# First expert layer in tiles of 128 rows instead of 256, rows standing in the array, second product in F32

## The reference, cut to what matters

```python
H, I, E, TOPK = 256, 688, 8, 2
logits = xf @ router_w.T
top_vals, top_idx = jax.lax.top_k(logits, TOPK)
top_w = jax.nn.softmax(top_vals, axis=-1)
combine = jnp.sum(jax.nn.one_hot(top_idx, E, dtype=xf.dtype) * top_w[..., None], axis=1)
for e in range(E):
    h = jax.nn.silu(xf @ Wg[e].T) * (xf @ Wu[e].T)
    y = h @ Wd[e].T
    out = out + combine[:, e:e + 1] * y
```

## Time and profile before

| | us |
|---|---|
| median of 3 runs | 1885.77 (1878.61 to 1891.75) |
| profiled execution, time | 1884.27 |
| profiled execution, span | 1882.5 |
| mean granted TensorE clock over the span | 0.932 of 2.4 GHz |
| TensorE busy | 1668.8 (89%) |
| VectorE busy | 1283.6 (68%) |
| ScalarE busy | 763.4 (41%) |

### The profile page before, as it was taken

One profiled execution on the slowest core, in us unless ns is written; L12 is line 12 of the kernel. 1 busy time (PEld: TensorE's weight loads), 2 busy tenths in 40 slices (PEclk: granted clock), 3 DMA queues, 4 the chain that ended last, 5 costly groups with the idle time before them and its releaser, 6 DMA issues. The chain is left out here.

```text
span 1882.5 us, 29054 instructions
## 1 busy us (share of the span) xinstructions
PE 1668.8 (89%) x9602; PEld 1163.0 (62%) x9602; DVE 1283.6 (68%) x2381; ACT 763.4 (41%) x1996; POOL 930.2 (49%) x815
## 2 busy tenths in 40 slices
PE   5999978999999999999999968899999289978890
PEld 4677744555555556555555644899999267755780
DVE  5688767777777777877777545687777756665333
ACT  3100103444444444444444423566665156642220
POOL 0477747777777788887775530232331000000536
PEclk9999978999999999999999986899999599988895
DMA  6434352212222222122220002765662420000343
GB/s 192 131 69 97 68 143 79 71 56 66 76 76 76 76 76 63 49 76 76 76 72 10 14 23 93 202 206 191 197 192 95 156 57 0 0 12 28 110 116 105
DMA packets 92020, 168.14 MB, mean 89 GB/s; under 512 B 45729, under 2 KB 70533, under 8 KB 87085
## 3 DMA queue, kind: packets, MB, share of 16 engines
q1 hardware_dynamic: 84077, 147.41, 26.6%
q0 software_dynamic: 7808, 19.02, 3.8%
HBM read 134.91 MB, written 29.53 MB: 87 GB/s over the span
## 5 line engine op out<-in xcount | busy, mean ns | idle before, releaser
L896 ACT ACTIVATE R<-banks 128x400 f32<-128x400 f32 x768 | 326.6, 510 | 318.1 <-PE banks L930 317.3
L712 DVE TENSOR_REDUCE PM<-banks 128x2 f32<-128x964 f32 x320 | 360.9, 1133 | 137.3 <-PE banks L689 137.2
L750 POOL TENSOR_TENSOR EA<-EA,R 128x400 f32<-128x400 f32 x288 | 306.1, 1063 | 118.8 <-ACT R L896 105.4
L930 PE MATMUL banks<-QS,KH 128*128 128x400 f32 x768 | 288.9, 376 | 2.6 <-DMA QB<-ML 2.6
L930 PE MATMUL banks<-QB,KB 128*128 128x400 f32 x768 | 265.6, 346 | 0.0
L730 DVE TENSOR_TENSOR banks<-banks,R 128x400 f32<-128x400 f32 x320 | 183.8, 574 | 27.9 <-ACT R L896 26.7
L539 POOL TENSOR_TENSOR arena<-arena 96x400 f32<-96x400 f32 x128 | 141.4, 1125 | 116.4 <-DVE arena L514 116.1
L182 PE MATMUL banks<-e_xh,e_split 128*116 128x256 f32 x960 | 194.5, 286 | 3.9 <-DVE e_xl L1702 3.9
L940 PE MATMUL banks<-R,KV 128*64 128x400 f32 x960 | 187.5, 512 | 0.0
L930 PEld LDWEIGHTS banks<-QS,KH 128*128 128x128 f32 x768 | 145.2, 189 | 54.7 <-issue 38.4
L689 PE MATMUL banks<-KH,QS 64*128 64x482 f32 x320 | 160.4, 502 | 17.2 <-DVE PM L712 7.7
(11 more groups left out here) (285 smaller groups left out, 3452.2 us busy)
## 6 DMA issues: line engine op xcount, KB each, us to landing
m_stage_u<-in_m_up SPq DMA_DIRECT2D x20, 1392.0 KB
arena<-in_ctx_T SPq DMA_DIRECT2D x16, 1444.0 KB, 6.2
m_stage_d<-in_m_down SPq DMA_DIRECT2D x20, 696.0 KB
QS<-queries SPq DMA_DIRECT2D x16, 800.0 KB, 6.6
queries<-q_out_h SPq DMA_DIRECT2D x64, 100.0 KB, 2.4
queries<-q_out_l SPq DMA_DIRECT2D x64, 100.0 KB, 2.4
QB<-queries SPq DMA_DIRECT2D x16, 400.0 KB, 8.4
arena<-recips SPq DMA_DIRECT2D x32, 200.0 KB
```

The lines of the kernel that those rows point to most:

```text
L712: nc.vector.tensor_reduce(PM[:, 2 * i:2 * i + n], banks[:, k:k + n, 0:KW], AX.X, ALU.max).then_inc(red_done, 1)
L750: nc.gpsimd.tensor_tensor(out, first, tile_of(n, 1), ALU.add).then_inc(odd_sum, 1)
L896: nc.scalar.activation(tile_of(n, o), psum[ring_bank(score_tile(b, n, o))][:, 0:CH], ACT.Exp).then_inc(exp_done, 1)
L930: last = nc.tensor.matmul(out, lhs[r][:, keys], heads[:, o], start=lhs is KH, stop=lhs is KB)
```

## The change

The first expert layer works in tiles of 128 rows (`TOK0`), so `most_tiles(8, 128)` = 32 tiles, each with one gather and one scatter of 128 rows. Each tile still loads its expert's up and down weights whole, in one DMA each, of unchanged shape; there are now three buffers of each. The rows (high and low) stand in the array and the up weights move, 348 of a projection's 696 columns at a time ("halves", index c): per tile 2 halves x 2 projections x 2 x 3 = 24 matmuls of 348 columns. ScalarE and VectorE split the up weights in four pieces per tile. The hidden values, 128 rows x 348, come out in F32 with rows on partitions, are turned by 6 transposes per tile, are moved to SBUF by ScalarE in F32 (`hidden_out`), and stand in the array against the unsplit F32 down weights (6 F32 products of 256 columns per tile). The splits of the down weights and of the hidden values are gone. The diff, cut to its core (`...` marks what is left out):

```diff
+TOK0 = P
...
 class GatedWeights:
-    BUFS, NU, TR, NT = 2, 2, 116, 6
+    BUFS, NU, TR, NT = 3, 2, 116, 6
...
-            d = Dispatch(core, ctx, stage, dram, "m0_", X, ident, E0, TOK, False, normed)
+            d = Dispatch(core, ctx, stage, dram, "m0_", X, ident, E0, TOK0, False, normed)
...
+    tag, U, PARTS = "e0_", 2, 2
+    PT, PC = NT // PARTS, TR * NT // PARTS
+    UB, TB, XB, YB = 0, NU * PARTS, NU * PARTS + PARTS, NU * PARTS + PARTS + 1
...
+        def stage_part(k, i):
+            return stage_u[k % BUFS][:, i % KD, :, part_of(i // KD)]
...
+        UPS = KD * PARTS
...
             def _(sp):
-                def load(k, u):
+                def up_of(k):
                     e = weights.expert_of(sp, d.tile_expert, k)
                     if k >= BUFS:
-                        sp.wait_ge(ul_ready, k + 1)
-                    weights.load_up(sp, e, u)
+                        sp.wait_ge(ul_ready, (k - BUFS + 1) * UPS)
+                    weights.load_up(sp, e, k)
+                    return e
+
+                def down_of(k, e):
                     if k >= BUFS:
-                        sp.wait_ge(dl_ready, k * NT + NT)
-                    weights.load_down(sp, e, u)
-
-                sp.wait_ge(x_in[0], 32)
+                        sp.wait_ge(down_done, (k - BUFS + 1) * PARTS)
+                    weights.load_down(sp, e, k)
+
+                sp.wait_ge(x_in[0], 16)
+                e = up_of(1)
                 for k in range(1, tiles):
-                    load(k, k % BUFS)
+                    following = up_of(k + 1) if k + 1 < tiles else None
+                    down_of(k, e)
+                    e = following
...
             def _(pe):
...
+                def up(k, c):
+                    pe.wait_ge(xl_ready, k + 1)
+                    pe.wait_ge(ul_ready, k * UPS + (c + 1) * KD)
+                    if k >= 1:
+                        pe.wait_ge(h_ready, (k - 1) * PARTS + c + 1)
+                    u = k % U
                     for n in range(NU):
-                        last = split_products(nc, psum[(u * NT + t) % HB][0:TR, n * TOK:(n + 1) * TOK],
-                                              [(UH[u][:, q, n, cols], UL[u][:, q, n, cols], xh[u][:, q, :], xl[u][:, q, :])
+                        last = split_products(nc, psum[UB + c * NU + n][:, 0:PC],
+                                              [(xh[u][:, q, :], xl[u][:, q, :], UH[u][:, q, n, part_of(c)], UL[u][:, q, n, part_of(c)])
                                                for q in range(KD)])
                     last.then_inc(up_ready, 1)
...
+                def turn_hidden(k, c):
+                    pe.wait_ge(h_ready, k * PARTS + c + 1)
+                    if k >= 1:
+                        pe.wait_ge(ht_ready, (k - 1) * PARTS + c + 1)
+                    for t in range(PT):
+                        last = nc.tensor.transpose(psum[TB + c][0:TR, t * TOK0:(t + 1) * TOK0], HF[:, c, t * TR:(t + 1) * TR], ident[:, :])
+                    last.then_inc(hid_turned, 1)
+
+                def down(k, c):
+                    pe.wait_ge(ht_ready, k * PARTS + c + 1)
+                    if c == 0:
+                        pe.wait_ge(down_in[k % BUFS], k // BUFS * 16 + 16)
+                        if k >= 1:
+                            pe.wait_ge(y_done, k)
+                    u = k % U
+                    for t in range(c * PT, (c + 1) * PT):
+                        last = nc.tensor.matmul(psum[YB][:, 0:D], HT[u][:, t, :], stage_d[k % BUFS][:, t, :], start=t == 0, stop=t == NT - 1)
                     last.then_inc(down_done, 1)
...
+                for k in range(tiles):
+                    up(k, 0)
+                    if k >= 1:
+                        turn_hidden(k - 1, 1)
+                        down(k - 1, 0)
+                    up(k, 1)
+                    if k + 1 < tiles:
+                        turn(k + 1)
+                    if k >= 1:
+                        down(k - 1, 1)
+                    turn_hidden(k, 0)
...
             def _(act):
...
+                for k in range(tiles):
+                    following = k + 1 < tiles
+                    if following:
+                        for i in range(KD):
+                            weights_high(k + 1, i)
+                    gate(k, 0)
+                    if k >= 1:
+                        hidden_out(k - 1, 1)
+                    if following:
+                        for i in range(KD, UPS):
+                            weights_high(k + 1, i)
+                    gate(k, 1)
+                    if following:
+                        rows_high(k + 1)
+                    hidden_out(k, 0)
```

More of the change, by code:

```diff
@@ L1532, in gated_experts, with part_of, split_part @@
         added = core.sem(tag + "added")
[L1534 to L1543, removed]
+        def part_of(c):
+            return slice(c * PC, (c + 1) * PC)
+        def stage_part(k, i):
+            return stage_u[k % BUFS][:, i % KD, :, part_of(i // KD)]
+        def split_part(W, k, i):
+            return W[k % U][:, i % KD, :, part_of(i // KD)]
+        UPS = KD * PARTS
         with nc.Block() as block:
@@ L1570, in send @@
                 def send(k):
[L1571 to L1574, removed]
+                    pool.wait_ge(y_done, k + 1)
+                    pool.indirect_dma_start(results[:, :], bass.IndirectOffsetOnAxis(d.target[:, k:k + 1], 0),
+                                            ys[k % U][:], None).then_inc(stored[k % U], 16)
                 for k in range(1, XBUFS):
@@ L1608, in up @@
                     last.then_inc(up_ready, 1)
[L1610 to L1620, removed]
-                    last.then_inc(down_done, 1)
@@ new lines, in _ @@
+                turn(0)
+                for k in range(tiles):
[9 more added lines that the diff above has]
+                    turn_hidden(k, 0)
+                k = tiles - 1
+                turn_hidden(k, 1)
+                down(k, 0)
@@ L1660, in step @@
[L1660 to L1667, removed]
-                        act.wait_ge(h_ready, k * NT + (HB + t + 1))
-                        act.wait_ge(down_done, k * NT + (t + 1))
-                        nc.scalar.activation(HH[u][:, t, :], HF[:, (u * NT + t) % HB, :], ACT.Copy).then_inc(hh_ready, 1)
-                    for t in range(NT + 1):
-                        if t < NT:
-                            gate(t)
-                        if t >= 1:
-                            high(t - 1)
-                        if not is_last(k):
-                            un, mn = next_of(u, m)
-                            for part in range(KD + 1):
-                                if ACT_AT[part] == t:
-                                    weights_high(k + 1, un, mn, part)
-                            if t == 2:
-                                rows_high(k + 1, un)
@@ L1685, in _, with weights_high @@
-                ACT_AT = (0, 1, 3)
-                for part in range(KD):
-                    weights_high(0, 0, 0, part)
-                rows_high(0, 0)
-                weights_high(0, 0, 0, KD)
-                steps(act, step)
+                def weights_high(k, i):
+                    if i == 0:
+                        act.wait_ge(up_in[k % BUFS], k // BUFS * 16 + 16)
+                        if k >= U:
+                            act.wait_ge(up_ready, (k - U + 1) * PARTS)
+                    nc.scalar.activation(split_part(UH, k, i), stage_part(k, i), ACT.Copy).then_inc(w_hi, 1)
@@ new lines, in _ @@
+                for i in range(UPS):
+                    weights_high(0, i)
+                rows_high(0)
+                for k in range(tiles):
[4 more added lines that the diff above has]
+                    gate(k, 0)
+                    if k >= 1:
+                        hidden_out(k - 1, 1)
[6 more added lines that the diff above has]
+                    hidden_out(k, 0)
@@ L1752, in _, with rows_low @@
[L1752 to L1760 removed]
+                def rows_low(k):
+                    v.wait_ge(xh_ready, k + 1)
+                    nc.vector.tensor_tensor(xl[k % U][:], psum[XB][:, 0:KD * TOK0].rearrange("p (k t) -> p k t", k=KD),
+                                            as_f32(xh[k % U][:]), ALU.subtract).then_inc(xl_ready, 1)
@@ new lines, in sums_out @@
+                def sums_out(k):
+                    v.wait_ge(down_done, (k + 1) * PARTS)
+                    if k >= U:
+                        v.wait_ge(stored[k % U], k // U * 16)
+                    nc.vector.tensor_copy(ys[k % U][:], psum[YB][:, 0:D]).then_inc(y_done, 1)
+                for i in range(KD):
+                    weights_low(0, i)
+                rows_low(0)
+                for i in range(KD, UPS):
+                    weights_low(0, i)
+                for k in range(tiles):
+                    following = k + 1 < tiles
+                    if following:
+                        for i in range(KD):
+                            weights_low(k + 1, i)
+                    hidden(k, 0)
```

(9 more changed lines are left out.)

182 lines of the change are left out of this document (52 added, 130 removed).

## The result

The changed kernel takes 2006.05 us (median of 4 runs, 1999.26 to 2008.85) against 1883.48 for the kernel before: 1.0641 times as long, 95% interval 1.0592 to 1.0689. The profiled execution took 1999.26 us with a span of 1997.5, 115 us more than the one of before.

The account below looks back on a forecast made before the run. Four DMA engines carrying the down loads bound it: 6.9 + 4.0 + 0.8 to 0.9, with loss 12.9 us a tile; 1 + 31 x 12.9 + 8 = 409 us, 114 more than before, 1998 us; range 1945 to 2025.

Parts of the forecast that it names:

- The bound of the kernel before: First expert layer: four full DMA engines, with TensorE close behind, set the period of 13.6 to 14.0 us.
- The price of the down load: One tile's 696 KB down load on its four DMA engines: at 103 GB/s, 6.9 us.
- The loss of 1.1 us a tile: Four engines, kernel before: the period's missing 1.1 to 1.4 us, taken as loss where queues alternate; assumed again after.
- TensorE's work: First expert layer after the change: 7.4 us a tile, 32 tiles, 236 us, against 263 us before.
- The chain inside a tile: Gate, `rows_high`, `rows_low` after the second up half: some 1.4 us plus hand-overs, covered by TensorE's other work.
- The cap of 8.1 us for compute: First expert layer after the change: compute alone would go at 7.4 to 8.1 us a tile.
- rival 1: Down loads take four other engines each time; compute decides at 8.1 us a tile: 1861 us, chance 0.06.
- The third buffer: Weight loads: depth adds no capacity, as the four engines already had a queue with two buffers; it keeps them fed.
- Rival 2: Loads slower than compute but cheaper than forecast, 10.5 to 11.8 us a tile: about 1945 us, chance 0.09.
- Rival 3: TensorE's clock falls towards 1.2 GHz when it idles, priced at 14 us a tile: 2032 us, chance 0.08.
- Rival 4: Only splitting and matmuls are halved, not loads; effects cancel at 9.2 us a tile: 1884 us, chance 0.05.
- the signs: Loop after the change: up loads every 12.7 to 13.4 us, DMA share 0.5 to 0.6, TensorE busy under 65%.

Follow-up runs that it names:

- padded kernel before: The kernel before the change, with down weights padded with zero rows from 116 to 128 partitions: 1867.98 us, 0.9942 times the kernel before.
- the run with half the weights: The changed kernel loading only slices 0 to 2 of each tile's down weights, used twice, on 116 partitions: 1886.67 us in one run.
- the padded kernel: The changed kernel with down weights padded with zero rows from 116 to 128 partitions, three buffers: 1836.73 us, 0.9758 times the kernel before.
- the two DMAs of 58 partitions: The changed kernel with each down load issued from SP as two DMAs, partitions 0 to 57 and 58 to 115: 2178.85 us in one run.

## Why the prediction was right

The forecast was 1998 us, from 12.9 us a tile on four full DMA engines. Measured: 2006.05, and 1999.26 in the profiled execution, with 12.76 us a tile.

- The bound of the kernel before. That four engines, and not TensorE alone, set its pace was argued from stretches at 0.31 and 0.26 with loads outstanding. The padded kernel before shows it: 13.25 us a tile instead of 13.6 to 14.0, and 12 us less; and the four are never without a packet in the 230 us. TensorE stood closer than was said: 108 x 0.12 + 0.44 is 13.4 us, not the 13.1 written, and 13.25 is measured.
- The price of the down load, 6.9 us on its four engines: half of it measured 3.6 for 3.45 in the run with half the weights. On two engines 118 partitions would by this price take 14.0 us, 7.1 more; measured from first queued load to read back they cost 200.7 us for 31 tiles, 6.5. What shrinks there is the loss: (607.0 - 9)/31 = 19.3 us a tile, against 14.0 + 4.0 + 0.85 = 18.9.
- The loss of 1.1 us a tile. 11.8 of the 12.76 us are explained by the uncontended prices, 0.96 remain. It is no idle time, since the four always have a packet in flight; it lies in longer packets, on average 0.29 us for one of a down load in the loop against 0.24 in tile 0's, alone. That queues taking turns lengthen them was only argued; two buffers, with less in the queue, lost slightly less (399.7 us from first load to read back against 406.3), which fits but doesn't show it. The term itself was taken over from the kernel before (1.1 to 1.4 us), and that it would be the same after the change had no other ground.
- TensorE's work, 7.4 us a tile: 7.28 measured, in the padded kernel, where nothing hides it. VectorE 5.1 us (139.46 x 7.28 / 200) and ScalarE 4.8 (130.70 x 7.28 / 200) a tile, priced 5.2 and 5.3.
- The chain inside a tile was said to be covered, and the padded kernel, with TensorE busy 200 of 200 us, shows it to be so. The cap of 8.1 us for compute was too careful, which is why rival 1's 1861 us would have been too high by 24.
- The third buffer was said to add nothing to the changed kernel, and adds nothing; that it is worth 20 us once the engines are free was not seen.
- Rival 1 (other engines each time) falls with the two DMAs of 58 partitions and with the packets of the changed kernel. The Trainium skill's rule that the prediction named ("DMA: Bandwidth & Descriptors", section "Why a DMA increments its semaphore by 16 and not by 1"), that a load from SP takes the lowest-numbered engines, agrees in that they are the same ones each time; that they are the lowest no trace shows. Rival 2 (the loss vanishes) had 11.8 us a tile as its upper end; 12.76 is above it. Rival 3's mechanism is there, and costs nothing: in the stretch at clock 0.50 six F32 instructions span 2.93 us instead of 1.46,

```profile
1380.85 2.93 PE L1626 MATMUL banks<-m_stage_d,e_HT 116*128 116x256 f32 x6 [2.52 <-ACT e_HT L1672]
```

but the four engines are never without a packet meanwhile, so nothing is lost by it. Rival 4 is true in its first half: the loads move whole.
- Two of the signs were missed by a little. TensorE was to be busy under 65% and is busy 71%, since part of its work runs at half clock and takes longer (242.33 us in 340, 9.1 a tile, against 7.28 at full clock). The DMA share was to be 0.5 to 0.6 and is 0.61.
- The end: 401 us were forecast from the first queued load to the last landing, and 8 from there to the read back. The last packet of a down load ends at 1571.90, so it is 398.6 and 7.7: 406.3 for 409.

So both the mechanism and the size came out. The step with the least behind it was the loss, and it came out at 0.96 us for 1.1.

## What to carry to other kernels

A low mean share of the DMA engines doesn't mean that DMA has room: look at windows of 1 to 2 us while a load is outstanding, and where the share stands at a plain fraction (0.25, 0.13) over several of them in a row, a few engines carry it all. One window alone can mislead: the padded kernel before also has 0.25 from 1302 to 1304 us, but there it is 0.49 in the first us and 0.00 in the second. Give weight tiles 128 partitions, even if zero rows fill them up: here 10% more bytes saved 169 us, and turned a change that cost 6.4% into one that gains 2.4%. Before tiles are made smaller, multiply what is loaded per tile by the new number of tiles, on the engine that carries most of it.

## What the runs showed of the hardware

A load of 116 partitions from SP ran on four DMA engines (share 0.25, 103 GB/s), one of 118 or of 58 on two (0.13, 49 to 53 GB/s), and always on the same ones, beside other loads on the rest. With all 16 engines in use the rate depended on the partitions of a load: 333 to 345 GB/s at a share of 0.91 to 0.94 with 128 partitions, 274 to 277 at 1.00 to 1.01 with 112. Down loads of 116 partitions from GpSimd used all engines, at 285 GB/s, where from SP they used four. TensorE's granted clock fell to 1.2 GHz in the loop after TensorE had stood idle (idle from 1378.33, the clock down from about 1380.4 to 1387.3) and returned while it worked; on average over the loop it was 0.88. It had no effect on the time, because the loads were later still.
